# Self attention of a fused transformer kernel: order of scores, transposes, maxima and copies, and three operations moved to GpSimd

## What is computed

```python
h = _rms(x, w_ln1)
q, k, v = ((h @ w + b).reshape(B, S, 16, 16) for w, b in ((wq, bq), (wk, bk), (wv, bv)))
q, k = _rope(q, k)
scores = jnp.einsum('bqhd,bkhd->bhqk', q, k) * HEAD_DIM ** (-0.5)
scores = jnp.where(causal[None, None], scores, jnp.finfo(scores.dtype).min)
attn = jax.nn.softmax(scores, axis=-1)
ctx = jnp.einsum('bhqk,bkhd->bqhd', attn, v).reshape(B, S, N_HEADS * HEAD_DIM)
x = x + ctx @ wo
h = _rms(x, w_ln2).reshape(B * S, H)      # then the router and the experts
```

## Time and profile before

| | us |
|---|---|
| median of 3 runs | 1247.73 (1245.5 to 1248.54) |
| the profiled execution, its own time | 1244.87 |
| its span, first to last instruction | 1242.8 |

### The profile page before, as it was taken

The page is one execution under the profiler, slowest core; times in us unless marked ns, Lnnn a source line. Parts: engine busy times, 40 slices in busy tenths (PEclk is TensorE's granted clock), DMA queues, the critical chain, the costliest instruction groups (busy, mean ns, idle before and its releaser), DMA issues.

```text
span 1242.8 us, 21905 instructions
## 1 busy us (share of the span) xinstructions
PE 1179.6 (95%) x8530; PEld 768.3 (62%) x8559; DVE 917.5 (74%) x1718; ACT 505.3 (41%) x1141; POOL 393.2 (32%) x397
## 2 busy tenths in 40 slices
PE   6999999999999999999999989899999988999998
PEld 3664658999745555555766745564566665455556
DVE  3777976677677777778757798887866577777766
ACT  3523360111224333334453336653434353555553
POOL 1540215656305333334003330001534052433330
PEclk9999999999999999999999999999999999999999
DMA  4040141000065344443240000002532100533431
GB/s 150 2 161 22 49 148 39 1 1 2 5 218 161 119 119 119 116 117 105 94 150 1 3 15 1 2 1 60 168 128 92 61 19 1 151 113 113 123 119 56
DMA packets 41542, 97.18 MB, mean 78 GB/s; under 512 B 5446, under 2 KB 18246, under 8 KB 39392
## 3 DMA queue, kind: packets, MB, share of 16 engines
q1 hardware_dynamic: 41440, 95.79, 24.4%
HBM read 94.35 MB, written 1.42 MB: 77 GB/s over the span
## 4 chain that ended last, share of the span: by engine, by line
PE 76%; DVE 15%; issue 3%; ACT 3%; DMA 2%; POOL 1%; SPq 0%; DVEq 0%; ACTq 0%; POOLq 0%
PE PS L1461 9%; PE PS L1463 9%; PE PS L1462 9%; PE PS L1508 5%; PE PS L1510 5%; PE PS L1509 5%; PE PS L1074 3%; PE PS L1092 2%; PE PS L1271 2%; PE PS L306 2%; PE PS L1060 2%; PE PS L1062 2%; PE PS L1061 2%; PE PS L2259 1%; DVE small L577 1%
## 5 line engine op out<-in xcount | busy, mean ns | idle before, releaser
L1718 POOL TENSOR_TENSOR arena<-arena,m_g 128x512 f32<-128x512 f32 x142 | 196.7, 1406 | 351.6 <-DMA m_g<-gate_rows 344.1
L1461 PE MATMUL PS<-arena 128*128 128x512 f16 x608 | 230.7, 379 | 3.0 <-DVE arena L1656 2.4
L1462 PE MATMUL PS<-arena 128*128 128x512 f16 x608 | 230.7, 379 | 0.0
L1463 PE MATMUL PS<-arena 128*128 128x512 f16 x608 | 230.6, 379 | 0.0
L1508 PE MATMUL PS<-arena 128*128 128x256 f16 x608 | 166.3, 274 | 6.6 <-DVE arena L1671 5.0
L1510 PE MATMUL PS<-arena 128*128 128x256 f16 x608 | 166.3, 274 | 0.0
L1509 PE MATMUL PS<-arena 128*128 128x256 f16 x608 | 166.2, 273 | 0.0
L1611 ACT ACTIVATE arena<-PS 128x512 f32<-128x512 f32 x112 | 66.8, 597 | 226.6 <-PE PS L1463 219.9
L1659 DVE SCALAR_TENSOR_TENSOR arena<-arena,PS 128x512 f32<-128x512 f32 x112 | 76.8, 685 | 77.1 <-ACT arena L1611 75.9
L1671 DVE TENSOR_TENSOR arena<-arena 128x512 f16<-128x512 f32 x142 | 128.5, 909 | 2.2 <-ACT arena L1622 1.8
L1463 PEld LDWEIGHTS PS<-arena 128*128 128x128 f16 x608 | 59.5, 98 | 71.9 <-issue 0.3
(11 more groups left out here) (282 smaller groups left out, 2223.1 us busy)
## 6 DMA issues: line engine op xcount, KB each, us to landing
w_stage<-in_up SPq DMA_DIRECT2D x80, 256.0 KB, 3.0
m_g<-gate_rows SPq DMA_DIRECT2D x70, 256.0 KB, 4.1
arena<-in_heads SPq DMA_DIRECT2D x16, 1088.0 KB, 5.3
w_stage<-in_down SPq DMA_DIRECT2D x80, 128.0 KB, 2.1
m_g<-gate_rows SPq DMA_DIRECT2D x17, 512.0 KB, 4.0
m_g<-gate_rows SPq DMA_DIRECT2D x6, 448.0 KB, 3.9
m_g<-gate_rows SPq DMA_DIRECT2D x6, 384.0 KB, 4.1
m_g<-gate_rows SPq DMA_DIRECT2D x6, 320.0 KB, 4.1
```

Source lines behind the costliest of these rows:

```text
L1461: pe.matmul(to, w_hi, x_hi, start=(k == 0), stop=False)
L1462: pe.matmul(to, w_lo, x_hi, start=False, stop=False)
L1463: ins = pe.matmul(to, w_hi, x_lo, start=False, stop=(k == KT - 1))
L1718: pool.tensor_tensor(p, p, m_g[:, st // 2 % 2, st % 2, :], ALU.mult).then_inc(s.c, 1)
```

## The change

In TensorE's queue the scores of step t + 2 now stand ahead of the transposes of step t; the filler matmuls and their wait for the copy stand ahead of both. In VectorE's queue the maxima of step t + 2 stand ahead of the reciprocals and the copy of step t. GpSimd gets a queue of its own for the stage, `pool_self`: it normalises each tile, spreads the inverses (all but the last tile's) and adds the new tile to the tokens. ScalarE waits for the transposes of step t - 2 ahead of the exponentials of step t, because the scores no longer stand behind them. New semaphores: `inv` (inverses there) and `mixed` (the tile's sum there).

```diff
@@ pe_self: turned(t)
                 if t:
                     pe.wait_ge(s.pt, t)
-                    if t % SA_OF_Q == 2 or t in (1, 4):
-                        pe_warm(3 if t % SA_OF_Q == 2 else 4, 2)
                 pe.wait_ge(s.p, t + 1)
@@ values(t)
                     if bq >= 2:
-                        pe.wait_ge(s.x2, bq - 1)
+                        pe.wait_ge(s.mixed, bq - 1)
@@ the loop of pe_self
             for t in range(SA_STEPS):
-                turned(t)
+                if t % SA_OF_Q == 2 or t in (1, 4):
+                    pe.wait_ge(s.pt, t)
+                    pe_warm(3 if t % SA_OF_Q == 2 else 4, 2)
                 if t + SA_AHEAD < SA_STEPS:
                     pe_scores(t + SA_AHEAD)
+                turned(t)
@@ new
+        def pool_self():
+            def normed(i):
+                pool.wait_ge(ln.rstd, powers_before[5] + 1)
+                pool.tensor_scalar(xn[:, i, :], x[:, i, :], meanvar[:, i, 0:1], rstd[:, i:i + 1],
+                                   ALU.subtract, ALU.mult).then_inc(ln.xn, 1)
+            def spread(bq):
+                pool.wait_ge(s.inv, bq + 1)
+                if bq:
+                    pool.wait_ge(s.oneT_ps, bq)
+                pool.tensor_copy(sa_one.rearrange("p (h c) -> p h c", h=H), over(small[:, bq % QT, 2, :], 2, HD)).then_inc(s.one, 1)
+            def added(bq):
+                pool.wait_ge(s.mixed, bq + 1)
+                pool.tensor_tensor(x[:, bq, :], x[:, bq, :], xn[:, bq, :], ALU.add).then_inc(s.x2, 1)
+            normed(0)
+            for bq in range(B * QT - 1):
+                normed(bq + 1)
+                spread(bq)
+                if bq:
+                    added(bq - 1)
+            pool_pow(s.ssq, 1, rms_r[:], rms_e[:], s.rr, 0)
+            added(B * QT - 2)
+            pool_pow(s.ssq, 2, rms_r[:], rms_e[:], s.rr, 1)
+            added(B * QT - 1)
@@ act_self
                 act.wait_ge(s.mx, t + 1)
+                if t >= 2:
+                    act.wait_ge(s.pt_ps, t - 1)
@@ dve_self: reciprocals(bq)
-                if bq:
-                    dve.wait_ge(s.oneT_ps, bq)
-                me.link(dve, dve.reciprocal(small[:, bq % QT, 2, :], small[:, bq % QT, 1, :]))
+                if bq >= 2:
+                    dve.wait_ge(s.one, bq - 1)
+                ins = dve.reciprocal(small[:, bq % QT, 2, :], small[:, bq % QT, 1, :])
+                if bq < B * QT - 1:
+                    ins.then_inc(s.inv, 1)
+                    return
+                me.link(dve, ins)
+                dve.wait_ge(s.oneT_ps, bq)
+                dve.wait_ge(s.one, bq)
@@ added(bq)
-                me.link(dve, dve.tensor_tensor(xn[:, bq, :], xn[:, bq, :], PS[:, 6 + bq % QT, 0:D], ALU.add))
-                dve.tensor_tensor(x[:, bq, :], x[:, bq, :], xn[:, bq, :], ALU.add).then_inc(s.x2, 1)
+                dve.tensor_tensor(xn[:, bq, :], xn[:, bq, :], PS[:, 6 + bq % QT, 0:D], ALU.add).then_inc(s.mixed, 1)
+                dve.wait_ge(s.mixed, bq + 1)
@@ the loop of dve_self
             for t in range(SA_STEPS):
+                if t + SA_AHEAD < SA_STEPS:
+                    dve_maxima(t + SA_AHEAD)
                 if t % SA_OF_Q == SA_OF_Q - 1:
                     reciprocals(t // SA_OF_Q)
                 turned(t)
-                if t + SA_AHEAD < SA_STEPS:
-                    dve_maxima(t + SA_AHEAD)
-                if t % SA_OF_Q == 1:
-                    dve_normed(5, t // SA_OF_Q)
```

More of the change, by code:

```diff
@@ L215, in build @@
                Sems("pre1", "h low logit e t"),
-               Sems("pre2", "hT z zT_ps ms r qkv biased copied qr qrT_ps qhi qT s mx p pt_ps pt one oneT_ps oneT v pv o y_ps x2 "
+               Sems("pre2", "hT z zT_ps ms r qkv biased copied qr qrT_ps qhi qT s mx p pt_ps pt inv one oneT_ps oneT v pv o y_ps mixed x2 "
                     "ssq rr z2 z2T_ps h low logit e t"),
@@ L1694, in dve_ffn @@
                     dve_routed(own["dve"], st)
+            if n == 2:
+                dve.wait_ge(pre[2].x2, NT)
             for i in range(NT):
@@ L2322, in pool_values @@
                     ins.then_inc(s.v, 1)
+        def pool_self():
+            pool, s = nc.gpsimd, pre[2]
+            def normed(i):
[20 more added lines that the diff above has]
+            added(B * QT - 1)
         def act_self():
@@ L2441, in pool_pre2 @@
             pool_values(me)
-            for part in range(2):
-                pool_pow(pre[2].ssq, part + 1, rms_r[:], rms_e[:], pre[2].rr, part)
+            pool_self()
         def dve_pre2():
```

## The result

The changed kernel takes 1256.4 us (median of 6 runs, 1254.07 to 1259.48), the kernel before 1246.03 in the same comparison: a ratio of 1.0084, 95% interval 1.0068 to 1.0099. It is slower, by 10.4 us; the sum had said 8.5. The profiled execution has a span of 1252.7, 9.9 more than before, and its own time is 1254.44.

What follows compares the result with a forecast made beforehand. The prediction took the order of waits between two nearly full engines, TensorE and VectorE, as the bound in layer 2's self attention. Head 4.2, periods 3.8 and tail 0.5 sum to +8.5 on 1247.73, forecasting 1256.2 us, range 1245 to 1261.

Steps and rivals of the forecast that it cites:

- Head: Start of layer 2's self attention, scores 1 to the transposes of t = 6: 16.16 us now, 20.3 after, +4.2.
- Periods: Each batch of eight steps in the stage: 21.44 us now, +1.3 with pauses, three times, +3.8 in all.
- A: The residual addition on VectorE, once per tile: falls from 1.26 to 0.92 us as the addition to x leaves.
- W: Burst of filler matmuls on TensorE at places 2 and 6 and t = 1 and 4; three fillers take 0.64 us.
- pauses at changes of shape: Pauses on TensorE where transposes directly follow the values matmuls: two places a period, +0.20 us.
- Tail: Behind the last steps, GpSimd's addition of tile 6 meets VectorE's tokens: +0.5 us, bounds 0 and +0.9.
- GpSimd elsewhere: GpSimd's moved operations within the stage: cost taken as 0, with +2.3 us as the bound.
- collision rival: Rival: VectorE's square waits for GpSimd's addition, 2.3 us on top: 1258.5, up to 1261 with upper pauses; chance 0.15.
- the M in front of the copy costs 1.13: Period on VectorE: the maximum now ahead of the copy out of PSUM costs 1.13 us; the removed addition returns 0.34.
- (c): VectorE does the maxima of t + 2 ahead of the copy of t, delaying what the next transposes and fillers await.
- TensorE is fed: Rival: copy at place 5 (places 0 to 7 per batch) in time keeps TensorE busy; 1241.1 us, chance 0.16.
- The orders cancel: Rival: maxima fill VectorE's idle time, so periods cost 0 and the head about +2: 1249.7 us, chance 0.19.

Runs made afterwards that it cites:

- x10: The changed kernel with x9's fillers, and GpSimd's additions of tiles 6 and 7 moved behind both of its powers; ratio 0.9988.
- x2: The kernel before with its old orders; only normalising, spread of inverses and addition to x moved to GpSimd; ratio 0.9984.
- x3: The kernel before with only TensorE's new order (scores ahead of transposes) and ScalarE's wait, nothing on GpSimd; ratio 1.0089.
- x5: The changed kernel with fillers still ahead of the scores but written into these scores' bank, so without the wait for the copy; ratio 1.0029.
- x6: The changed kernel without the filler matmuls in the loop of 32 steps and without their waits for the copy; ratio 1.0000.
- x9: The changed kernel with fillers at t = 1, 2 and 4 alone, written into the scores' bank without a copy wait; ratio 0.9980.
- x1: The kernel before with both new orders and ScalarE's wait, nothing moved to GpSimd; ratio 1.0128.
- x7: The kernel before without the filler matmuls in the loop, the wait for the copy kept; ratio 1.0025.

## Why the prediction was right, and where it was not

The time, 1256.4, is 0.2 from the forecast. Against the kernel before of the same comparison it is +10.4 against a sum of +8.5, so this agreement is luck: the sum was 1.9 short, and the median it was added to, 1247.73, was 1.7 above the 1246.03 of the comparison. The direction and the mechanism, longer waits for the copy, are not luck; they stand term by term below.

- **Head.** +4.2 said, +3.99 measured. The step holds: the burst at t = 4 was named as the reason.
- **Periods.** 22.74 said (22.54 and 0.20 for pauses), 22.93 measured; three times, +3.8 said and +4.47 measured. The steps stand one by one in the timeline: a maximum to the next VectorE work 1.14 (807.30 to 808.44), the copy 1.13, A 0.91 (809.57 to 810.48), the maximum 1.14, the copy to the end of W 1.93 (811.62 to 813.55). The mis-sized term is that of the pauses at changes of shape, 0.4 in place of 0.2 in a period, 0.6 over three: for instance, scores of 256 keys start 0.10 later behind a burst than counted (800.11 to 801.61 against 0.76 + 0.64).
- **Tail.** +0.5 said, +0.40 measured, and x10 shows the mechanism. The section "Key points" of the page GPSIMD Engine Reference (the Trainium skill) names the conditions under which the two contend, a two-port mode or two SBUF inputs. This case's numbers agree where they bear on it: beside the square, which reads SBUF twice, GpSimd's addition took 0.96 in place of 0.73, and a copy from PSUM beside GpSimd's normalising kept its 1.21 (811.62). The tokens read SBUF and slowed from 1.14 to 1.53; whether they run in a two-port mode no trace here shows.
- **GpSimd elsewhere.** 0 said, and x2 agrees. The square in A takes its 0.42 as before, while GpSimd's addition takes 0.96, not 0.73: GpSimd was held, not VectorE, as the prediction took it. The collision rival falls. The spread took 0.40 (said 0.4 to 0.9); the normalising 1.22, above my bound, and it cost nothing.
- **The cause as it was worded.** The prediction says that "the M in front of the copy costs 1.13". As a term of the sum that is right, as a cause it is not: x3 takes the M away and the period grows, to 24.08 from 23.27. The step that failed is (c), which judged one order with the other held fixed at the old one. The loss comes from TensorE's order with its fillers: with scores in front, T and the copy come late, and a burst that waits for that copy holds the next scores. x5 replaces this wait by the one that the scores have anyway and gets 1.64 of 22.93 back.
- **Rivals.** "TensorE is fed" needed the copy at place 5 to come in time; it did not, and only x6, x9 and x10, which have no burst there, reach 20.5. "The orders cancel" is refuted by x1.
- **Not foreseen.** The clock fell once in the stage, behind a wait of 2.13, +1.56 in the profiled execution. The sum has no such term, and it is most of the 1.9 that it was short. How often it falls in the stage without a profile can't be read from single times; the mean granted clock of the six timed runs was 0.995 to 0.997, that of the profiled kernel before 0.999, and the two slowest (1259.48 and 1257.62) have 0.995.

That the change of the clock in the stage is due to the longer waits is argued, not shown: x3 has waits as long (2.17) and no fall in its stage, and of x9 and x10, with the same loop and the same wait, only x10 has one.

## What to carry to other kernels

A filler or any other instruction that waits for a buffer should not stand ahead of work that doesn't need that buffer: in an in-order queue its wait becomes theirs. Moving it to a buffer that the next work waits for anyway removed 1.64 of a period of 22.93 with the same number of fillers. And two orders on two engines that feed each other have to be changed and judged together: the scores ahead, with their fillers, alone cost 2.6 us a period, the maxima ahead alone 10.1, both 1.8.

## What the runs showed of the hardware

**The clock.** In the profiled executions the granted clock of TensorE fell to half (1.2 in place of 2.4 GHz) for 3.4 us at a time, or 6.8 and 13.6. One fall cost 1.56 us in the stage of the changed kernel and 1.14 in x10 (84.15 against 83.01 in x9). Whether it comes is not settled by the length of the wait ahead of it alone: it fell behind a wait of 2.13 us at t = 14 of the changed kernel and not behind 2.09 at t = 22 and 30, nor behind 2.17 in x3; it fell behind 1.87 at T(30) of x10 and not behind 1.86 at the same place of x6 and x9. Without fillers in the head it stayed down for 13.6 us in x7. In x6 and x9 the periods from t = 8 on have no fillers and kept the full clock, with waits up to 1.86; in x10 they did not all keep it.

**VectorE and GpSimd.** In the changed kernel the one that started first was not held. The square on VectorE started at 810.01 and took its 0.42; the addition on GpSimd started at 810.06 and took 0.96. In the tail the addition started first, at 842.66, and took 0.73; the tokens on VectorE started at 842.80 and took 1.53 in place of 1.14.
